# Value products of a vision transformer in five token groups instead of six, with moved splits, loads and zero fills

## What is computed

```python
h = tokens(x)                                                    # patches @ W_lin.T + b, class token, positions
h = h + attention(layernorm(h), w_q, w_k, w_v, w_o, rel_bias)    # 16 heads of 64, bias by relative position
h = h + moe(layernorm(h), router_w, w_gate, w_up, w_down, sw_*)  # 7 experts, the best 2 of a token, and a shared one
h = h + scan(layernorm(h), W_delta, b_delta, W_value, b_value)   # gated running state over the tokens
h = h + channel_mix(layernorm(h), W_r, W_k, W_v, mu_r, mu_k)
```

```python
v = shape(hidden_states @ w_v)              # 592 x 256 times 256 x 1024
ctx = jnp.einsum('bhqk,bhkd->bhqd', attn, v)
```

## Time and profile before

| | us |
|---|---|
| median of 3 runs | 316.23 (316.22 to 316.68) |
| profiled execution, whole | 318.52 |
| its span, first to last instruction | 316.5 |
| TensorE busy in the span | 304.6 (96%) |
| VectorE / ScalarE / GpSimd busy | 192.7 / 187.4 / 157.9 |
| granted TensorE clock | full throughout (0.999) |

### The profile page before, as it was taken

One profiled execution on the slowest core, in us unless ns is written; L12 is line 12 of the kernel. 1 busy time (PEld: TensorE's weight loads), 2 busy tenths in 40 slices (PEclk: granted clock), 3 DMA queues, 4 the chain that ended last, 5 costly groups with the idle time before them and its releaser, 6 DMA issues.

```text
span 316.5 us, 7394 instructions
## 1 busy us (share of the span) xinstructions
PE 304.6 (96%) x3094; PEld 278.9 (88%) x3094; DVE 192.7 (61%) x368; ACT 187.4 (59%) x324; POOL 157.9 (50%) x141
## 2 busy tenths in 40 slices
PE   8899999999999999999999999999999998999995
PEld 7776878889998999998999999999999998886673
DVE  1679135555654696747846776574838595736862
ACT  3485435756546685447597675847567463378761
POOL 6036013674442324464948686768585886200333
PEclk9999999999999999999999999999999999999999
DMA  7956226933000621549484848484757642000002
GB/s 246 412 138 188 77 75 198 276 134 119 2 4 2 199 68 68 183 144 292 133 288 117 285 116 278 145 267 162 265 167 223 198 157 85 22 4 0 1 0 81
DMA packets 32438, 46.03 MB, mean 145 GB/s; under 512 B 4272, under 2 KB 19728, under 8 KB 32400
## 3 DMA queue, kind: packets, MB, share of 16 engines
q1 hardware_dynamic: 30000, 41.71, 41.8%
q0 software_dynamic: 960, 2.43, 2.3%
q10 hardware_dynamic: 1440, 1.38, 1.4%
HBM read 38.22 MB, written 5.71 MB: 139 GB/s over the span
## 4 chain that ended last, share of the span: by engine, by line
PE 74%; DVE 8%; POOL 5%; ACT 4%; issue 3%; DMA 3%; SPq 1%; another core or an unknown queue 0%; DVEq 0%; POOLq 0%; ACTq 0%
PE ps L1578 19%; PE ps L1580 18%; PE ps L1579 18%; PE ps L1931 6%; PE ps L1731 3%; PE ps L1760 3%; PE ps L1600 3%; DMA v_region<-in_blocks 2%; PE ps L1593 2%; POOL v_region L569 2%; POOL w_lo L513 2%; DVE c_region L1021 2%; PE ps L1716 1%; DMA v_region<-expert_out,row_i 1%; DVE w_lo L1021 1%
## 5 line engine op out<-in xcount | busy, mean ns | idle before, releaser
L1578 PE MATMUL ps<-c_region,w_hi 128*128 128x224 f32 (+2 forms) x304 | 88.1, 290 | 1.2 <-DVE c_region L1021 1.1
L1579 PE MATMUL ps<-c_region,w_hi 128*128 128x224 f32 (+2 forms) x304 | 85.2, 280 | 0.0
L1580 PE MATMUL ps<-c_region,w_lo 128*128 128x224 f32 (+2 forms) x304 | 85.2, 280 | 0.0
L506 POOL TENSOR_TENSOR w_lo<-w_stage,w_hi 128x512 fp32r<-128x512 f32 x30 | 48.5, 1637 | 31.1 <-ACT w_hi L750 31.0
L1578 PEld LDWEIGHTS ps<-c_region,w_hi 128*128 128x128 f32 x304 | 58.1, 191 | 3.1 <-DVE c_region L1021 2.1
L1579 PEld LDWEIGHTS ps<-c_region,w_hi 128*128 128x128 f32 x304 | 58.1, 191 | 0.2
L1580 PEld LDWEIGHTS ps<-c_region,w_lo 128*128 128x128 f32 x304 | 58.0, 191 | 0.0
L750 ACT ACTIVATE w_hi<-w_stage 128x1024 fp32r<-128x1024 f32 (+1 forms) x42 | 49.7, 1196 | 2.6 <-DVE v_region L1423 2.6
L1021 DVE TENSOR_TENSOR c_region<-s_region,c_region 128x448 fp32r<-128x448 f32 (+1 forms) x44 | 37.4, 850 | 17.4 <-ACT c_region L877 11.6
L513 POOL TENSOR_TENSOR w_lo<-w_stage,w_hi 128x512 fp32r<-128x512 f32 x28 | 38.0, 1389 | 8.3 <-ACT w_hi L750 8.3
L1578 PE MATMUL ps<-xn_hi,w_hi 128*128 128x296 f32 x128 | 40.2, 314 | 0.9 <-DVE xn_lo L1021 0.7
(11 more groups left out here) (192 smaller groups left out, 604.4 us busy)
## 6 DMA issues: line engine op xcount, KB each, us to landing
w_stage<-in_w_gate SPq DMA_DIRECT2D x17, 512.0 KB, 4.9
w_stage<-in_w_up SPq DMA_DIRECT2D x17, 512.0 KB, 4.7
w_stage<-in_w_down SPq DMA_DIRECT2D x8, 1024.0 KB
expert_rows<-zeros SPq DMA_DIRECT2D x1, 1792.0 KB, 9.4
v_region<-in_blocks SPq DMA_DIRECT2D x6, 272.0 KB, 4.8
v_region<-expert_rows SPq DMA_DIRECT2D x1, 1344.0 KB, 8.2
expert_out<-v_region ACTq DMA_DIRECT2D x6, 224.0 KB, 4.7
w_stage<-in_w_v SPq DMA_DIRECT2D x1, 1024.0 KB, 7.3
```

The lines of the kernel that those rows point to most:

```text
L506: w = g.tensor_tensor(wl[:, r], ws[:, r], wh[:, r].bitcast(F32), ALU.subtract)
L1578: mm(o, a_h, b_h, start=start, stop=False)
L1579: mm(o, a_h, b_l, start=False, stop=False)
L1580: return mm(o, a_l, b_h, start=False, stop=stop)
```

## The change

- **Groups.** `VG` goes from 3 per chunk to 5 in all: images 0-2, 5-7, 9-11 and a piece of image 12, then 3, 4, 8 with a piece of 12, and 13-15 with a piece of 12; sizes 111, 111, 128, 114, 128. The torn image is put together by SP's moves (11 move DMAs instead of 8).
- **Gathers.** Groups 3 and 4 are not contiguous: SP copies their tokens, high and low part, from SBUF to SBUF into `xv` (a free part of c_region) with five DMAs, after the low part of chunk 1 (ln_lo 2). TensorE waits for all five (d_xv 80) ahead of group 3. For this `xh` and `xl` become one tensor, xn_split.
- **Places.** Groups 0 and 1 stand ahead of the query and key products, groups 2 and 3 in step 0, group 4 in step 1 ahead of that step's query and key products. The chunk-0 query and key products wait for ln_lo 1 and ln_rs 2 in place of ln_lo 2.
- **POOL.** The low halves of w_k and w_q start only after ln_lo 2; each split is made in two instructions of 512 columns.
- **Head.** DVE makes `embedded(0)` and `embedded(1)` ahead of the chunk-1 patch splits, and `centre(0, 0)` ahead of the last two of them.
- **Fill and loads.** The zero fill becomes four of 448 KB from a wider source (2048-byte pieces); fills and loads of the shared expert are issued one by one, each after a set attention step (sc_ev 5 to 15).

```diff
-VG = 3
+VG = 5
+        V_FIRST = (0, 5, 9, 3, 13)
+        V_PAIR = (0, 3, 5, None, 7)
+        V_ROWS = (VR, VR, P, 3 * T + T - 2 * GIVEN, P)
+        xv = cr[:, 2 * PW:2 * PW + 4 * KD * P]
...
+            sp.wait_ge(s["ln_lo"], 2)
+            gather_tokens(3, (3 * T, 2 * T), (8 * T, T), (TORN * T + torn(2).start, T - torn(2).start))
+            gather_tokens(4, (13 * T, 3 * T), (TORN * T + torn(1).start, GIVEN))
...
+            fill_rows(0)
             sp.wait_ge(w_lo[0], 1)
             sp.wait_ge(s["up_lo"], 3)
+            sp.wait_ge(s["sc_ev"], 5)
             load("g0", 0)
+            sp.wait_ge(s["sc_ev"], 6)
+            fill_rows(1)
             sp.wait_ge(w_lo[1], 1)
-            sp.wait_ge(s["up_lo"], 2)
+            sp.wait_ge(s["sc_ev"], 7)
             load("u0", 0)
...
             for p in (2, 1, 0):
                 h = 0 if p == 2 else 1
                 pool.wait_ge(w_hi[p], 2)
-                g.tensor_tensor(columns(wl, p, h), columns(ws, p, h), columns(wh, p, h).bitcast(F32),
-                                ALU.subtract).then_inc(s["up_lo"], 1)
+                if p == 1:
+                    pool.wait_ge(s["ln_lo"], 2)
+                for k in range(KD):
+                    o = p * W1 + k * INNER + h * (INNER // 2)
+                    r = slice(o, o + INNER // 2)
+                    w = g.tensor_tensor(wl[:, r], ws[:, r], wh[:, r].bitcast(F32), ALU.subtract)
+                w.then_inc(s["up_lo"], 1)
...
-            for u in range(3, 2 * VG):
-                value(u // 2, u % 2)
-            pe.wait_ge(s["ln_lo"], 2)
+            value(1, 1)
...
             for c in range(C):
+                pe.wait_ge(s["ln_lo"], c + 1)
+                pe.wait_ge(s["ln_rs"], 2)
                 for j in range(2):
                     project(0, c, j)
...
                 if t + 2 < 2 * HP:
+                    if t == 1:
+                        for n in range(2):
+                            value(4, n)
                     project(t // 2 + 1, t % 2, 0)
                     project(t // 2 + 1, t % 2, 1)
-                    if t < 2:
-                        for g in ((VG, VG + 1), (VG + 2,))[t]:
+                    if t == 0:
+                        for g in (2, 3):
+                            if g == 3:
+                                pe.wait_ge(s["d_xv"], 80)
                             for n in range(2):
                                 value(g, n)
```

More of the change, by code:

```diff
@@ L162, in vit_tower, with torn, v_tokens, v_rows_of @@
         v_all = vreg[:, :]
-        KIND = (0, 1, 2, 2, 0, 1)
-        def v_rows(g):
-            return VR if KIND[g] < 2 else T2
-        def v_half(g, n):
[L172 to L179, removed]
+        TORN = 12
+        GIVEN = P - 3 * T
+        V_FIRST = (0, 5, 9, 3, 13)
+        V_PAIR = (0, 3, 5, None, 7)
+        V_ROWS = (VR, VR, P, 3 * T + T - 2 * GIVEN, P)
+        xv = cr[:, 2 * PW:2 * PW + 4 * KD * P]
+        def torn(i):
+            return slice(i * GIVEN, min((i + 1) * GIVEN, T))
+        def v_half(g, n):
+            if V_PAIR[g] is None:
+                return sq[0:V_ROWS[g], n * 512:(n + 1) * 512]
+            o = V_PAIR[g] * INNER + n * 512
+            return v_all[0:V_ROWS[g], o:o + 512]
+        def v_tokens(g, k):
+            r = V_ROWS[g]
+            if g >= 3:
+                return (xv[:, o:o + r] for o in (2 * KD * P * (g - 3) + (i * KD + k) * P for i in range(2)))
+            return (x[:, k * NT + V_FIRST[g] * T:k * NT + V_FIRST[g] * T + r] for x in (xh, xl))
+        def v_rows_of(pair, r0, n):
+            return v_all[r0:r0 + n, pair * INNER:(pair + 1) * INNER]
         ctx_h, ctx_l = cr[:, 0:HP * N], cr[:, HP * N:2 * HP * N]
@@ L328, in v_bank @@
         def v_bank(g, n):
-            return 2 * (g % 2) + n if g < VG else 2 + n
+            return 2 * g + n if g < 2 else 2 + n
         def qk_bank(n):
@@ L374, in _, with gather_tokens @@
             sp.dma_start(tb[0:BUCKETS, :], table).then_inc(s["d_bias_in"], 16)
+            def gather_tokens(g, *pieces):
+                at = 0
+                for o, n in pieces:
+                    sp.dma_start(pat(xv, 2 * KD * P * (g - 3) + at, [P, 2 * KD], [1, n]).bitcast(F32),
+                                 pat(xs[:], o, [NT, 2 * KD], [1, n]).bitcast(F32)).then_inc(s["d_xv"], 16)
+                    at += n
             def part(p):
@@ L399, in _ @@
             sp.dma_start(part(2).rearrange("p (k n) -> p k n", k=HP), rows(w_o, HP)).then_inc(d_w[2], 16)
[L401 to L422, removed]
+            def evicted(g):
+                sp.wait_ge(s["v_ev_act"], g + 1)
+                sp.wait_ge(s["v_ev_dve"], g + 1)
@@ new lines, in move, with evicted_rows, move_torn @@
+            def move(c, pair, to, rows):
+                sp.dma_start(v_all[to:to + rows.shape[0], pair * INNER:(pair + 1) * INNER], rows).then_inc(d_vm[c], 16)
+            def evicted_rows(g, r0, n):
+                return v_rows_of(V_PAIR[g], r0, n) if V_PAIR[g] is not None else sq[r0:r0 + n, 0:INNER]
+            def move_torn(g, i):
+                r = torn(i)
+                move(1, 6, r.start, evicted_rows(g, 3 * T, r.stop - r.start))
+            evicted(0)
+            move(0, 1, 0, evicted_rows(0, T, MR))
@@ new lines, in _ @@
+            evicted(1)
+            move(0, 2, VR - MR, evicted_rows(1, T2 - MR, MR))
+            sp.wait_ge(s["ln_lo"], 2)
+            gather_tokens(3, (3 * T, 2 * T), (8 * T, T), (TORN * T + torn(2).start, T - torn(2).start))
+            gather_tokens(4, (13 * T, 3 * T), (TORN * T + torn(1).start, GIVEN))
+            sp.wait_ge(s["gap_set"], 4)
+            evicted(2)
+            move(1, 4, VR - MR, evicted_rows(2, T2 - MR, MR))
+            move_torn(2, 0)
+            evicted(3)
+            move(0, 1, T2, evicted_rows(3, 0, MR))
@@ L424, in load @@
+            move(0, 2, 0, evicted_rows(3, T, MR))
+            move(1, 4, 0, evicted_rows(3, T2, MR))
+            move_torn(3, 2)
+            evicted(4)
+            move_torn(4, 1)
+            move(1, 6, VR - MR, evicted_rows(4, T2 - MR, MR))
             def load(n, e, rows=KH):
@@ L497, in _ @@
             for pair in (PPC + 1, PPC + 2):
[L498 removed]
+                g.memset(v_all[0:VR, pair * INNER:(pair + 1) * INNER], 0.0).then_inc(s["gap_set"], 1)
             def half_low(n, e):
```

73 lines of the change are left out of this document (42 added, 31 removed).

## The result

The changed kernel takes 313.29 us (median of 10 executions, 312.39 to 315.43) where the kernel before takes 316.43 (10 executions on the same chip, 316.12 to 317.26): a ratio of 0.9914, 95% interval 0.9890 to 0.9938. By the medians it is faster by 3.1 us, by the ratio by 2.7; 5.2 were forecast, and 313.29 lies just outside the range that ended at 313.2. In four of the ten executions, at 314.35 to 315.43 us, the mean granted TensorE clock was 0.993 to 0.995; in the other six, 312.39 to 313.32 us, it was 1.0. The profiled one is of the four: 315.43 us, span 313.5.

The account below looks back on a forecast made before the run. TensorE, busy 304.6 of 316.5 us, was taken to bound the kernel, so gains came from its gaps: 1.00 + 3.13 - 0.1 + 0.45 + 0.76 = 5.24 us off 316.23 gives 311.0 us, range 310.3 to 313.2.

Parts of the forecast that it names:

- Change 1: Head: embedded ahead of VectorE's chunk-1 patch splits removes TensorE's wait ahead of the first mean, worth 1.00 us.
- Change 2: Chunk 1's layer norm: normal freed of GpSimd's split, 1.41 us; chunk 0's query/key products inside the wait, 1.72 us.
- rival A: Chunk 1's layer norm: normal is slow for another reason than GpSimd, so 1.41 us do not come; 312.4 us, chance 0.07.
- Change 3: Value groups, one fewer: steps 0 and 1 hold as many value matmuls as before, so nothing is added.
- Change 4: Step 0: added waits on ScalarE's eviction and the gathers cost a 0.1 us stall; gathers land 1.7 us ahead of need.
- rival C: Step 0: GpSimd's moved splits are slow and stall group 3 by 1.6 us, not 0.1; 312.5 us, chance 0.06.
- D: Rival, step 0: gathers cost 51 ns a packet and stall TensorE 3.9 us; 314.8 us, chance 0.04.
- E: Rival, step 0: gathers cost 101 ns, a read and a write each, stalling 12.0 us; 322.9 us, chance 0.04.
- Change 5: Step 1: query/key matmuls cover the last value eviction, so step 2's transposes no longer wait, worth 0.45 us.
- Change 6: Attention: spaced fills and loads no longer hold up an instruction fetch, worth 0.76 us; last load hidden by 9.6 us.
- Rival B: Attention: the 0.76 us instruction gap stays or turns up at another fetch; 311.8 us, chance 0.17.
- Rival F: Expert stage: starts at the same time, bound by a load, although attention ends earlier; about 316.2 us, chance 0.04.

Follow-up runs that it names:

- f3: dn12 with chunk 0's query and key products made to wait for chunk 1's low part (ln_lo 2) again; 315.23 us, ratio to before 0.9899.
- f4: dn12 with value group 4 put back behind step 1's query and key products, its eviction behind step 1's exponential; 313.92 us, ratio to before 0.9873.
- e1: Changed kernel with the down weights' load (dn) issued one attention step earlier, sc_ev 12 instead of 13; 310.87 us, ratio to before 0.9823.
- g3: Changed kernel with the dn load in two halves, the second one attention step later (sc_ev 14); 312.18 us, ratio to before 0.9846.
- dn12: The kernel run as e1: changed kernel with the dn load one attention step earlier; 310.87 us, and 311.20 us when repeated on another chip.
- e2: Changed kernel with the dn load issued one attention step later, sc_ev 14 instead of 13; 312.24 us, ratio to before 0.9873.
- e3: Changed kernel without any wait on an attention step ahead of fills and loads, so they run back to back; 314.69 us, ratio to before 0.9930.

## Why the prediction was wrong, point by point

**Change 1, 1.00 us: right.** The wait is gone; the mean came 0.71 us earlier although TensorE was half a us behind before in the products ahead of it (the same matmul starts at 8.21 us in before and at 8.70 in after). Undone, the wait is back with 0.93 us, and the time loses 1.6 +- 1.

**Change 2, 1.41 + 1.72 us: right in sum, its first part not shown in the time.** Between the first mean and chunk 1's products the shift grew by 3.92 - 0.71 = 3.21 us where 3.13 were forecast. `normal` went from 2.19 to 0.78 us, so rival A is out. But with GpSimd's splits put back the chain lost 0.67 us, perhaps because they are now cut in 512 columns and fall elsewhere; 1.41 is what that one execution of the old order showed. The other part is confirmed by f3: 1.84 us of wait.

**Change 3, nothing: right.** Nothing in the shifts asks for more; it was not undone by itself.

**Change 4, -0.1 us: right.** The splits took 1.25 us each (1.24 forecast), so rival C is out, and no wait showed on ScalarE's eviction. The gathers landed ahead of need, so D and E are out; but the forecast margin of 1.7 us was too large, since SP took 3.48 us to issue the five, not 2.3.

**Change 5, 0.45 us: right.** 0.52 us by the shifts (3.65 at the scores ahead of it, 4.17 behind), 0.45 by f4.

**Change 6, +0.76 us: the step that failed.** Before's gap went, as forecast, and TensorE was 5.37 us ahead at 61.65 us in the time of after (with a gap of 1.07 us in the profile of before that this is measured against, where 0.76 was counted). What failed is "spaced, one transfer at a time is in flight" and "hidden by 9.6 us". The second looked only at who reads the load's data. The load of 1024 KB fills the queues for some 4 us by itself, and the prediction's own reading of the earlier trace rows says what that does: the fetch waits. The question was then at which fetch each spaced transfer ends, and that was not asked. In the changed kernel dn meets one, for 1.92 us, and in the executions where the clock then falls another 1.4 us go (shift -2.90 at 84.57 us, -1.50 at 87.80). The shifts give the two groups of executions. At 84.57 us, with the gap over and the clock not yet down, TensorE is 2.90 us ahead: 316.4 - 2.9 = 313.5 us, close to the six executions at full clock, 312.39 to 313.32. At 87.80 us it is 1.50 us ahead, 314.9 us: the four others, 314.35 to 315.43. How long the gap was in the nine executions without a profile is not on record, so the first of these is an estimate.

Rival B had the mechanism ("turns up at another fetch"), at the price of the gap that was known, 0.76 us; that price was the second error, as a gap's length is not a property of the fetch. With B at the 2 to 3.5 us that runs of this study show, the range would have reached 314.5.

The Trainium skill, "Runtime: NRT & Kernel Launch", section Instruction fetch mechanics, says that an engine's sequencer fetches the next block of 16 KiB over a DMA queue of its own while it executes, and that this is mostly hidden. The transfers of 16 KiB on a queue of their own (q8) are what the traces show; some of them are not hidden, with gaps of 0.28 to 2.04 us in nine profiles. The prediction weighed the rule as a reason for the gap to stay; what e1 and g3 show is that such a transfer can wait for the packets of a load all the same.

**The comparison of before with its median.** The prediction set the span of the profiled execution, 316.5, beside the median of whole times, 316.23. The whole time of that execution was 318.52, 2.3 us above. It did no harm to the sum, as the excess lay late in the program: the second profile of before runs 0.15 us ahead of the first at 67 us, 1.17 at 144 and 1.75 at 268.

**Rival F** is out: in e1 the 5.95 us of shift at 67 us in the time of before are 5.55 at 200 us, behind the small gap at 72.30, and 5.96 at 268 us, where a wait on VectorE was 0.68 us instead of 1.09. So it is in part luck that dn12's 310.87 us lies 0.1 from the forecast: a dearer gap in before, the small gap and shorter late waits cancel.

## What to carry over

When transfers are moved, ask of each not only who waits for its data but which instruction fetch falls due behind it: look in the trace for the times at which the instruction queue moves, and place a long load so that it ends well ahead of the point where the bottleneck engine reaches a new block, or cut it in pieces. Since a one-step shift of one load was worth 2.4 us here by the medians and 2.9 by the ratios, more than most of the edits, it pays to try the neighbouring places on the chip. And profile the kernel before twice before a term is read from one gap or one slow instruction.

## What the runs showed of the hardware

- An instruction transfer can be held up by a load: in after it came at 82.19 us when the load was through at 82, in e1 at 78.75, with the load halved at 80.02. Full DMA engines do not always hold it up. In before, within 51 to 57 us, one begins while the fills keep the engines busy, and no gap follows:

```profile
q1 hardware_dynamic: 3398, 1.75, 100.3%
q8 instruction: 1, 0.02, 0.9%
```

What lets one pass and holds another was not found. TensorE resumed 1.2 to 1.5 us behind the end of the transfer in all gaps looked at (after 1.41 and 1.39, before 1.34, e2 1.33, e3 1.54 and 1.48, g3 1.43, f4 1.23), so a gap can be foretold from the transfer's end. That the transfer is TensorE's own is inferred from this regularity; the trace does not name an engine for it.
- After 1.92, 2.04 and 2.23 us of idle TensorE the granted clock stood at 0.50 (1.2 GHz), for about 3 us in after and f3 and about 7 in e3; after gaps of 1.06, 1.00 and 0.83 us it did not fall in these profiles. One execution of e2 without a profile has a mean clock of 0.995, so the length of the gap in one profile does not settle it for the kernel. After the 1.92 us gap 1.4 us were lost on top of it.
- SP took 0.70 us to issue each gather of 128 x 4 short pieces, where a bias transfer took 0.47. The gathers of 12 to 444 bytes a piece landed in 2.7 to 3.7 us in after and 3.5 to 4.7 in e2, where 3.1 was forecast from the rows of 128 to 148 bytes.
- Late waits of TensorE on VectorE differ by up to 0.7 us each between executions of one kernel (0.70 us at 145.23 us in the first profile of before, none in the second).
